# One squares product per step instead of two, weight casts on ScalarE, weights next to the transposed inputs, and a new order inside the step

## What is computed

```
h = layernorm(x) * (1 + ca) + sa
x = x + ga * attention(h)
h = layernorm(x) * (1 + cb) + sb
x = x + gb * ffn(h)          # silu(h Wg) * (h Wu), then Wd; inner size 1376
```

```
q, k = rope(h Wq), rope(h Wk);  v = h Wv;  dt = softplus(h Win + bias);  g = -dt * exp(A)
G = cumsum(g) inside a chunk
y_intra = ((q k^T) * exp(G_i - G_j), causal) @ (v * dt)
y_inter = (q * exp(G)) @ state,  state = k^T of the chunk before, decayed, @ (v * dt)
y = y_intra + y_inter
y = y / sqrt(mean(y^2) + eps) * gnorm * silu(h Wgate)
out = y Wo
```

## Time and profile before

| | |
|---|---|
| three runs | 1116.08, 1113.23, 1115.06 us, median 1115.06 |
| profiled execution | 1113.59 us, span 1111.8 us, mean granted TensorE clock 0.984 |
| PE busy | 1067.2 us, 96% of the span, 4680 products |
| PE weight loads | 808.9 us, 73% |
| DVE busy | 767.0 us, 69% |
| ACT busy | 550.8 us, 50% |
| POOL busy | 206.1 us, 19% |
| DMA | 70.89 MB, mean 64 GB/s |

### The profile page before, as it was taken

How to read it: one execution, slowest core, us unless ns; L and a number is a source line. 1 busy time by engine, 2 the same in 40 slices (tenths; PEclk the granted TensorE clock), 3 DMA queues, 4 the chain that set the end, 5 groups by cost and what they waited for, 6 DMA issues and landing times. The chain is left out here.

```text
span 1111.8 us, 14213 instructions
## 1 busy us (share of the span) xinstructions
PE 1067.2 (96%) x4680; PEld 808.9 (73%) x4680; DVE 767.0 (69%) x1492; ACT 550.8 (50%) x1133; POOL 206.1 (19%) x131
## 2 busy tenths in 40 slices
PE   4879999999999999999999999999999969999898
PEld 1757777777777777777777777777776449888786
DVE  5777786877787678868876887778676686434411
ACT  3445556665555666555666555566655434222300
POOL 3412211212221121122111222211121530000000
PEclk9989999999999999999999999999999979999999
DMA  6121301220131013112201320131031622111011
GB/s 223 58 69 49 124 30 38 75 75 19 38 113 38 19 38 113 38 28 83 96 19 38 97 54 19 38 113 38 19 95 24 204 99 72 49 45 57 29 38 38
DMA packets 37464, 70.89 MB, mean 64 GB/s; under 512 B 2936, under 2 KB 19576, under 8 KB 35520
## 3 DMA queue, kind: packets, MB, share of 16 engines
q1 hardware_dynamic: 36720, 70.16, 19.9%
q10 hardware_dynamic: 720, 0.43, 0.1%
HBM read 68.33 MB, written 2.24 MB: 63 GB/s over the span
## 5 line engine op out<-in xcount | busy, mean ns | idle before, releaser
L1299 POOL TENSOR_TENSOR q_sin<-q_sin,cst 128x512 f32<-128x512 f32 x64 | 82.8, 1293 | 390.9 <-ACT q_sin L751 390.9
L1292 POOL TENSOR_TENSOR dec<-dec,future 128x1024 f32<-128x1024 f32 x31 | 80.3, 2590 | 273.6 <-ACT expg L770 273.6
L848 ACT ACTIVATE work<-ps_y 128x512 f32<-128x512 f32 x64 | 38.4, 599 | 186.4 <-PE ps_y L673 185.6
L54 PE MATMUL ps_gt<-hT_hi,wg_hi 128*128 128x512 f32 x256 | 125.7, 491 | 3.7 <-DVE sg L986 3.7
L54 PE MATMUL ps_q<-hT_hi,wq_hi 128*128 128x512 f32 x256 | 125.5, 490 | 2.8 <-DVE q_cos L966 2.3
L54 PE MATMUL ps_o<-wo_hi,z_hi 128*128 128x512 f32 x260 | 104.1, 400 | 2.4 <-DVE z_lo L49 2.4
L55 PE MATMUL ps_o<-wo_lo,z_hi 128*128 128x512 f32 x260 | 103.4, 398 | 0.0
L56 PE MATMUL ps_o<-wo_hi,z_lo 128*128 128x512 f32 x260 | 103.0, 396 | 0.0
L56 PE MATMUL ps_q<-hT_hi,wq_lo 128*128 128x512 f32 x256 | 101.2, 395 | 0.0
L55 PE MATMUL ps_gt<-hT_lo,wg_hi 128*128 128x512 f32 x256 | 100.7, 393 | 0.0
L56 PE MATMUL ps_gt<-hT_hi,wg_lo 128*128 128x512 f32 x256 | 100.7, 393 | 0.0
(11 more groups left out here) (239 smaller groups left out, 2553.0 us busy)
## 6 DMA issues: line engine op xcount, KB each, us to landing
dec<-gT_dram SPq DMA_DIRECT2D x32, 512.0 KB, 5.4
raw_q<-wq_in SPq DMA_DIRECT2D x32, 256.0 KB, 2.7
raw_g<-wg_in SPq DMA_DIRECT2D x32, 256.0 KB, 2.9
raw_o<-wo_in SPq DMA_DIRECT2D x8, 1024.0 KB, 7.3
raw_pair<-wkv_in SPq DMA_DIRECT2D x8, 512.0 KB, 4.7
raw_pair<-wgu_in SPq DMA_DIRECT2D x6, 512.0 KB, 3.3
raw_gu<-wgu_in SPq DMA_DIRECT2D x5, 512.0 KB, 3.4
qT<-wmod_in SPq DMA_DIRECT2D x2, 1024.0 KB, 7.0
```

Of the source, the lines that this page charges most:

```text
L54: pe.matmul(out, w_hi, x_hi, start=first, stop=False)
L848: nc.scalar.activation(sq, ps_y[:], ACT.Square).then_inc(sq_done, 1)
L1292: nc.gpsimd.tensor_tensor(cells, cells, future[:].unsqueeze(1).broadcast_to([P, GRP * CPB, CHUNK]), ALU.add).then_inc(mask_done, 1)
L1299: nc.gpsimd.tensor_tensor(q2, q2, sinT, ALU.mult).then_inc(qsin_done, 1)
```

## The change

- **Folded squares.** ACT squares the lower and the upper 64 partitions of ps_y into two tiles of 64 partitions, `sq_low` and `sq_top`. DVE adds them (`sum_squares`, `sq_sum`), ACT rounds the sum into the lower half of `sq_parts` (`round_squares`), DVE writes the rest into its upper half. One product of ones with `sq_parts` takes the place of two.
- **Casts.** The high halves of head, key/value and output weights in the groups are made by ACT (Copy) and no longer by DVE. `split_o_hi` waits for `o_ready`.
- **Placement.** `wo_hi`, `wo_lo`, `wkv_hi`, `wkv_lo` are allocated from the right, next to `hT`.
- **Buffers.** `prob` and `z` are tiles of their own; `win_lo` too. `gated_y` now waits for `zlo_done`; the probabilities and squares no longer do.
- **Order.** PE: `y_product` stands ahead of `out_product`, `k_turn` after half of the g block, `square_sum` last. DVE: the probabilities of step t + 1 stand at the end of step t, ahead of `normed_z`; the low halves of the q weights stand with those of the gate weights, ahead of the cap; `wo_lo` stands there in step 0. ACT: weight casts follow the decays, then the gate's exponential, and in even steps the sigmoid stands ahead of `inverse_rms`.

```diff
-        wkv_hi, wkv_lo = (sb(n, [P, KT, 2 * D], F32R) for n in ("wkv_hi", "wkv_lo"))
-        wo_hi, wo_lo = (sb(n, [P, GRP, HID], F32R) for n in ("wo_hi", "wo_lo"))
+        wo_hi, wo_lo = (sb(n, [P, GRP, HID], F32R, "right") for n in ("wo_hi", "wo_lo"))
+        wkv_hi, wkv_lo = (sb(n, [P, KT, 2 * D], F32R, "right") for n in ("wkv_hi", "wkv_lo"))
...
-        work = sb("work", [P, GRP, CHUNK])
-        prob, z = work, work
-        sq = work[:].rearrange("p h i -> p (h i)")
-        sq_hi, sq_lo = sb("sq_hi", [P, HALF], F32R), sb("sq_lo", [P, HALF], F32R)
+        prob, z = sb("prob", [P, GRP, CHUNK]), sb("z", [P, GRP, CHUNK])
+        sq_parts = sb("sq_parts", [P, HALF], F32R)
+        sq_top, sq_low = sb("sq_top", [P // 2, HALF]), sb("sq_low", [P // 2, HALF])
+        sq_sum = sb("sq_sum", [P // 2, HALF])
...
 
                 pe.wait_ge(sqhi_done, g * 8 + (t + 1))
-                nc.tensor.matmul(ps_ss[:], ones[:], sq_hi[:], start=True, stop=False)
                 pe.wait_ge(sqlo_done, g * 8 + (t + 1))
-                nc.tensor.matmul(ps_ss[:], ones[:], sq_lo[:], start=False, stop=True)\
+                nc.tensor.matmul(ps_ss[:], ones[:], sq_parts[:], start=True, stop=True)\
                     .then_inc(ss_ready, 1)
...
                     q_block(g, t)
+                y_product(g, t)
                 out_product(g, t)
+                if project:
+                    g_block(g, t, 0, 2)
                 if c == 1 and next_batch:
                     k_turn(g, b)
-                y_product(g, t)
                 if project:
-                    g_block(g, t, 0, KT - 1)
-                square_sum(g, t)
-                if project:
-                    g_block(g, t, KT - 1, KT)
+                    g_block(g, t, 2, KT)
                 if c == 0 and next_batch:
                     kv_batch(g, b)
+                square_sum(g, t)
 
             def tail(g, t):
                 b, c = t // 2, t % 2
...
+            def round_squares(g, t):
+                act.wait_ge(sqsum_done, g * 8 + (t + 1))
+                nc.scalar.activation(sq_parts[0:64], sq_sum[:], ACT.Copy).then_inc(sqhi_done, 1)
...
-                nc.scalar.activation(sq, ps_y[:], ACT.Square).then_inc(sq_done, 1)
-                nc.scalar.activation(sq_hi[:], ps_y[:], ACT.Square).then_inc(sqhi_done, 1)
+                nc.scalar.activation(sq_low[:], ps_y[0:64], ACT.Square)
+                nc.scalar.activation(sq_top[:], ps_y[64:128], ACT.Square).then_inc(sq_done, 1)
...
+            def split_head_hi(g, j):
+
+                act.wait_ge(wh_loaded, g * 128 + 32 * (j + 1))
+                nc.scalar.activation(wq_hi[:, j], raw_q[:], ACT.Copy)
+                nc.scalar.activation(wg_hi[:, j], raw_g[:], ACT.Copy).then_inc(wh_hi_done, 1)
+
+            def split_kv_hi(g):
+                act.wait_ge(kv_loaded, g * 16 + 16)
+                nc.scalar.activation(wkv_hi[:], raw_kv[:], ACT.Copy).then_inc(kv_hi_done, 1)
+
+            def split_o_hi(g):
+
+                act.wait_ge(o_ready, g * 8 + 1)
+                act.wait_ge(wo_loaded, g * 16 + 16)
+                nc.scalar.activation(wo_hi[:], raw_o[:], ACT.Copy).then_inc(wo_hi_done, 1)
...
                 squares(g, t)
+                round_squares(g, t)
                 if c == 1:
                     copy_kT(g, b)
                 decays(g, t + 1)
-                inverse_rms(g, t)
+                if next_group and 1 <= t <= GRP:
+                    split_head_hi(g + 1, t - 1)
+                if next_group and t == GRP + 1:
+                    split_kv_hi(g + 1)
+                if t == 0:
+                    split_o_hi(g)
                 exp_gate(g, t)
-                split_z_hi(g, t)
-                sigmoid(g, t)
                 if c == 0:
+                    sigmoid(g, t)
+                    inverse_rms(g, t)
                     copy_v(g, b)
+                    split_z_hi(g, t)
                     exp_g(g, b)
+                else:
+                    inverse_rms(g, t)
+                    sigmoid(g, t)
+                    split_z_hi(g, t)
 
             def tail(g, t):
                 b, c = t // 2, t % 2
...
-            def probabilities(g, t, tail=False):
-
-                b, c = t // 2, t % 2
-                dest = prob_tail if tail else prob
-                if tail and t == 4:
-                    dve.wait_ge(sg_done, g * 8 + 8)
-                if not tail:
-                    dve.wait_ge(zlo_done, g * 8 + (t + 1))
+            def probabilities(g, t):
+
+                tile = t % NT
                 dve.wait_ge(s_ready, g * 8 + (t + 1))
                 dve.wait_ge(dec_done, g * 8 + (t + 1))
                 for h in range(GRP):
                     last = nc.vector.scalar_tensor_tensor(
-                        dest[:, h], ps_s[:, h * P:(h + 1) * P], scal[:, t, 1, h:h + 1],
-                        dec[:, b % 2, h, c], ALU.mult, ALU.mult)
+                        prob[:, h], ps_s[:, h * P:(h + 1) * P], scal[:, tile, 1, h:h + 1],
+                        dec[:, tile // 2 % 2, h, tile % 2], ALU.mult, ALU.mult)
                 last.then_inc(prob_done, 1)
 
             def cross_probabilities(g, t):
@@ -1173,15 +1192,20 @@
                         expg[:, h], ALU.mult, ALU.mult)
...
+            def sum_squares(g, t):
+
+                dve.wait_ge(sq_done, g * 8 + (t + 1))
+                nc.vector.tensor_tensor(sq_sum[:], sq_low[:], sq_top[:], ALU.add).then_inc(sqsum_done, 1)
+
             def gated_y(g, t):
 
                 half = t // 4
-                dve.wait_ge(sqhi_done, g * 8 + (t + 1))
-                split_lo(nc.vector, sq_lo[:], sq, sq_hi[:]).then_inc(sqlo_done, 1)
-                dve.wait_ge(sqlo_done, g * 8 + (t + 1))
+                dve.wait_ge(zlo_done, g * 8 + (t + 1))
                 dve.wait_ge(sg_done, g * 8 + (4 * half + 4))
                 nc.vector.tensor_tensor(z[:], ps_y[:].rearrange("p (h i) -> p h i", h=GRP),
                                         sg[:, half, :, rows_of(t)], ALU.mult).then_inc(zz_done, 1)
+                dve.wait_ge(sqhi_done, g * 8 + (t + 1))
+                split_lo(nc.vector, sq_parts[64:128], sq_sum[:], sq_parts[0:64]).then_inc(sqlo_done, 1)
 
             def normed_z(g, t):
...
                 heads, keys = next_group and 1 <= t <= GRP, next_group and t == GRP + 1
-                probabilities(g, t)
+                gate(g, t - 1)
                 if c == 1:
                     rotate_k(g, b, t)
-                gate(g, t - 1)
                 rotate_q_cos(g, t)
                 if c == 0:
                     cross_probabilities(g, t)
-                if heads:
-                    split_head_hi(g + 1, t - 1)
-                if keys:
-                    split_kv_hi(g + 1)
+                sum_squares(g, t)
                 rotate_q_add(g, t)
+                gated_y(g, t)
                 add_out(g, t)
-                gated_y(g, t)
                 if heads:
                     split_head_lo_g(g + 1, t - 1)
+                    split_head_lo_q(g + 1, t - 1)
                 if keys:
                     split_kv_lo(g + 1)
                 if c == 0:
                     copy_scalars(g, b)
                 if t == 0:
-                    split_o_hi(g)
+                    split_o_lo(g)
+                cap(g, t)
+                probabilities(g, t + 1)
                 normed_z(g, t)
-                cap(g, t)
-                if heads:
-                    split_head_lo_q(g + 1, t - 1)
                 split_z_lo(g, t)
-                if t == 0:
-                    split_o_lo(g)
 
             def tail(g, t):
                 b, c = t // 2, t % 2
                 if t == 4:
...
                     guard_gate(0)
+                sum_squares(g, t)
                 gated_y(g, t)
```

More of the change, by code:

```diff
@@ L198, in block_attention, with sb @@
     with ExitStack() as ctx:
-        def sb(name, shape, dt=F32):
-            return ctx.enter_context(nc.sbuf_tensor(name, shape, dt))
+        def sb(name, shape, dt=F32, side=None):
+            return ctx.enter_context(nc.sbuf_tensor(name, shape, dt, side=side))
         def ps(name):
@@ L249, in block_attention @@
         silu_c = sb("silu_c", [P, KT * B])
-        win, win_hi, win_lo = (w[:].rearrange("p (k h) -> p k h", k=KT) for w in (q_cos, sq_hi, sq_lo))
+        win, win_hi = (w[:].rearrange("p (k h) -> p k h", k=KT) for w in (q_cos, sq_parts))
         rows = cross[:, 1, 0:2 * H].rearrange("p (r h) -> p r h", r=2)
@@ L329, in block_attention @@
         sq_done = sem("sq_done")
+        sqsum_done = sem("sqsum_done")
         sqhi_done = sem("sqhi_done")
@@ L661, in scores, with y_product @@
                                  start=True, stop=True).then_inc(s_ready, 1)
-            def y_product(g, t, tail=False):
+            def y_product(g, t):
                 b, c = t // 2, t % 2
@@ L671, in y_product @@
                 pe.wait_ge(prob_done, g * 8 + (t + 1))
-                weights = prob_tail if tail else prob[:]
```

(10 more changed lines are left out.)

15 lines of the change are left out of this document (5 added, 10 removed).

## The result

The changed kernel takes **1121.92 us** (median of 4 runs, 1121.34 to 1122.92) beside 1115.53 for the kernel before: ratio **1.0069**, 95% interval 1.0053 to 1.0085, so slower by 0.5 to 0.9%: 6.4 us between the medians, 7.7 by the ratio. The forecast was 1120.5.

The account below looks back on a forecast made before the run. TensorE, full at full clock, bounds the loop; the dependent chain bounds the tail. Waits 20.0, product -13.8, placement -2.5 and tail +2.5 sum to +6.2 us; forecast 1120.5, range 1102 to 1128.

Parts of the forecast that it names:

- The removed product: TensorE, full part: one 512-column product less in each of 60 steps, 0.23 us each, 13.8 us off.
- The odd chain: Odd steps with casts: from k transposes through casts, low halves and z_lo, TensorE starts at 7.90 us, against 7.17 without waiting.
- The wait of 0.8: TensorE before the first ps_o product of steps 2, 4 and 6: 0.8 us each with restart, 2.4 per group.
- Output weights, 0.4: Wait at step 1 from ACT's 2048-column cast at t = 0, priced 2.2 us (1.9 the lower estimate): about 0.4 per group.
- signs that I had listed for being wrong: Loop shows no idle, another product waits (y, k transposes, or square_sum for sq_lo), or the granted clock falls in the loop.
- 0.3 to spare: At t = 1, square_sum's margin for sq_lo; POOL's hold on DVE there could cost up to 1 us per group.
- Steps without a wait: Loop steps 3, 5, 7 and 0 show no wait; two steps take 25.35 us without a wait, 26.15 with one.
- Placement, -2.5: Moving wo and wkv shortens 720 products by 0 to 9 ns, 0 to 6.5 us; 2.5 us taken off.
- placement does nothing: Rival: location of wo and wkv changes nothing, sum +8.7, total 1122 to 1124; chance 0.20.
- Tail, +2.5 with 4.8 as the end: Last four steps: chain up to 1.2 us longer each, separate buffers giving some back; 0 to 4.8, 2.5 on.
- The chain fits: Rival: the odd steps' chain stays under TensorE's 7.17 us, so most waits go; spread 1100 to 1112, chance 0.30.
- DVE held by POOL: Rival: DVE's added addition is slowed by POOL's q_sin in odd steps of the loop: +7, 1127, chance 0.10.

Follow-up runs that it names:

- E3: Changed kernel with the old squares (two full squares, one subtraction, two products) in the loop and the last group's first four steps: 1128.47 us, ratio 1.0114.
- E1: Changed kernel with ACT's casts of the head and key/value weights ahead of the kT copy in odd steps: 1109.48 us, ratio 0.9948.
- E9: Changed kernel with the edits of E1 and E4, plus the inverse root ahead of the sigmoid on ACT in step 0: 1099.82 us, ratio 0.9864.
- E7: Changed kernel with the edits of E1 and E4, plus the output weights' high half cast by DVE again: 1107.12 us, ratio 0.9932.
- E2: Changed kernel without the placement, wo and wkv allocated where the kernel before had them: 1120.88 us, ratio 1.0052.
- E4: Changed kernel with the old squares and two square products in the four tail steps alone: 1116.22 us, ratio 1.0020.

## Why the prediction was right, and where its terms were not

**The sum.** Forecast +6.2. By the profiles: product -15.9, waits +18.8, placement 0, tail +4.9, after the tail -0.6: +7.2, without the prologue's chance. Measured 6.4 between the medians, 7.7 by the ratio (5.9 to 9.5). The direction rests on the odd chain, which was right. That the total is so close is luck: placement and tail were 4.9 too low together, product, waits and the rest 3.9 too high.

**The removed product, 60 x 0.23 = 13.8.** Sized too low: two steps without a wait are 25.27 long and not 25.80, 0.265 per product, 15.9 in all. E3 puts it back and pays 0.26 in the steps without a wait, though its second product starts 0.24 after the first (450.01 and 450.25). Followed product by product, E3's step 3 falls behind the changed kernel's by the other 0.03 within the q block. Why it does is open.

**The odd chain, 7.90.** Right, term by term, in step 3. From the transposes (443.46) I had kT at 0.42, decays 0.68, the second cast done at 3.04, the low halves at 3.08, `normed_z` 5.67 to 6.36, `z_hi` 6.39, `z_lo` 7.07 to 7.76, TensorE 7.90. The rows above have 0.42, 0.70, 3.01, 3.04, 5.62 to 6.30, 6.34 (449.80), 6.99 to 7.68, 7.84. `normed_z` starts right behind the probabilities. The wait of 0.8 measured 0.53, 0.74 and 0.62 by step length, 1.89 per group where I had 2.4. That of step 2 is the shortest since TensorE has already waited for the squares of step 1 between the transposes and there (next paragraph); before step 6 the one cast of double width and its low half take 1.04 and 1.23 (471.34 and 472.42), where the two pairs of step 3 take 1.14 and 1.29. E1 shows the chain to be the cause.

**Output weights, 0.4.** The first wait of step 1 is that: its product starts at 413.12, 1.19 after the y product (411.93) and not 0.86, plus 0.08 for the restart. The cast took 1.90, my lower estimate, with which my sum would have had a wait of only 0.1; other pieces of the chain were 0.2 longer and TensorE came 0.1 earlier, so the match of 0.4 is in part luck. That the root stands behind the sigmoid was foreseen too, and is what E9 undoes. What I missed is a second wait of 0.29, in front of step 1's square sum. It is one of the signs that I had listed for being wrong (another product waits, `square_sum` for `sq_lo`), so this part of the mechanism was wrong:

```profile
418.37 0.69 DVE L49 TENSOR_TENSOR sq_parts<-sq_sum,sq_parts 64x512 fp32r<-64x512 f32 x1
419.20 0.47 PE L687 MATMUL ps_ss<-sq_parts,ones_r 128*128 128x512 f32 x1
```

The product ahead of it starts at 418.77, so it could have gone at 419.00. I had named this spot, with "0.3 to spare", under POOL's hold on DVE. The `z_lo` of step 0 comes late, and all of DVE's row in step 1 stands behind it: E9 moves `z_lo` and both waits go, with POOL's hold still there. E7 moves the cast to the engine that casts faster, and the waits grow.

**Steps without a wait.** 0, 3, 5 and 7 have none, as said. Two steps without one take 25.27 where I had 25.35, and with one 25.80 to 26.01 where I had 26.15.

**Placement, -2.5: failed.** I took a difference of 6 to 9 ns in the length of a product for location. E2 settles it at nothing, and the mean length of these products moves by 2 to 4 ns between kernels of one placement, without a trace in the time. The rival "placement does nothing" held as a mechanism, and its total, 1122 to 1124, is met better than the forecast's 1120.5 (1121.92 and 1123.24). The Trainium skill, page "SBUF — State Buffer", section "SBUF: two separate sides", says that TensorE's ports never wait on anyone; these runs agree.

**Tail, +2.5 with 4.8 as the end: failed, 4.9.** I gave back part of the chain for separate buffers, as the squares need not wait for `z_lo` any more. They never did wait: before, ACT squares at 884.54, 0.10 after `ps_y` ends. And I priced the DVE pieces at 0.69. In step 6 they are longer:

```profile
893.15 0.89 DVE L1198 TENSOR_TENSOR sq_sum<-sq_low,sq_top 64x512 f32<-64x512 f32 x1 [3.42 <-ACT sq_top L850]
894.74 0.98 DVE L49 TENSOR_TENSOR sq_parts<-sq_sum,sq_parts 64x512 fp32r<-64x512 f32 x1
895.87 0.47 PE L687 MATMUL ps_ss<-sq_parts,ones_r 128*128 128x512 f32 x1 [2.26 <-DVE sq_parts L49]
```

The first of these is longer still in step 5, beside POOL's additions to x:

```profile
879.10 5.07 POOL L400 TENSOR_TENSOR x<-x,raw_o 128x512 f32<-128x512 f32 x3
879.73 1.63 DVE L1198 TENSOR_TENSOR sq_sum<-sq_low,sq_top 64x512 f32<-64x512 f32 x1
```

Over steps 5 to 7 these additions and low halves are together 2.1 us longer than the 0.67 and 0.69 they take where POOL is still; of the low halves before, in the same steps, one is longer, by 0.3. So part of the tail's loss is the rival of POOL's hold, which I had priced for the loop only. In step 6, from the y product to the out product it is 5.42 (890.76 to 896.18) against 3.74 before (883.32 to 887.06): 1.7 more, the product's 0.23 already off, where I had 1.2 as the most. E4 takes 4.0 of the 4.9 us back by its profile.

**Rivals.** *The chain fits*: no, but E1 and E9 show how near it was; one exchange of neighbours in ACT's row turns 0.7% slower into 0.5% faster. *DVE held by POOL*: the +7 did not come, and the odd chain was not touched, but the hold is there, in the tail as above and in the loop. In step 1 of the changed kernel it lies in the row that is late:

```profile
412.75 2.40 POOL L1311 TENSOR_TENSOR dec<-dec,future 128x1024 f32<-128x1024 f32 x1 [11.90 <-ACT expg L769]
414.30 1.14 DVE L983 TENSOR_TENSOR kr<-q_cos 128x256 f32<-128x256 f32 x1
```

The sum of squares behind it takes 0.97, and 0.68 in step 0, where POOL is still. This alone is as much as the second wait, 0.29. So E9 shows that the hold costs nothing once `z_lo` is early; what part it has in the second wait of the changed kernel is not shown, as no run takes it away.

**Range.** The terms' bounds, added straight, go from 1109 to 1129 on 1113.59; I had 1113 to 1127 from them. The measured time lies within either.

## What to carry to other kernels

A product removed ahead of a wait gives nothing, and a reordering that makes room for it must be costed for what now stands ahead of the waited result: here up to 0.7 us of excess in a chain of fourteen instructions, three times in each of seven groups, ate 13 of the 16 us gained, and the waits of step 1 more than the rest. Put work without a deadline into the hole ahead of an instruction that waits for another engine, not behind it. The engine's busy share said nothing on that here, and a slower engine that is free earlier can beat a faster one (E7). Read waits from the length of whole steps, since idle marks leave out part of them.
